# Attention stages with small heads: scores in pairs of different 64-row halves, maxima in pairs behind them

## The chip, the cores and the metric

One Trainium2 chip, one of its cores. The metric is the device time of one execution in microseconds: median of the runs, lower is better. Engines are called TensorE (PE), VectorE (DVE), ScalarE (ACT), GpSimd (POOL) and SyncE (SP).

## The reference

Eight layers on x of 4 x 512 tokens and 256 channels, each adding to x what it makes of the normalised x: a selective scan, a mixture of experts, rotary attention, the same experts, then two attentions of which the kernel makes the stages pattern and latent, other experts, grouped attention with a memory, and the other experts again. What matters here is three attentions whose heads are small:

- rotary and pattern: 16 heads of width 16 each, queries and keys of 512 tokens a batch, four batches. Of each head `softmax(q k^T * scale) v`, where the maximum over the keys is taken off before the exponential.
- grouped: 4 x 8 query heads of width 8 on 8 shared key heads, the same softmax, then a mix with what a memory gives.

## The kernel before, in words

Nine stages run one after the other: mamba, ffn0, rotary, ffn0, pattern, latent, ffn1, grouped, ffn1. Every engine runs its own list of instructions, and semaphores join them. In the three stages named above, the class `Heads` (L931 to L1180) lays out the attention.

**Stacks.** A group is four heads of one batch. There are 16 groups in rotary and in pattern, 32 in grouped. For each, the q of four heads stands in `q_stack` in rows of the 128 partitions: a head takes 64 rows in rotary and pattern (two heads to a tile, two tiles), and 32 in grouped (four heads in one tile). The rows hold high and low parts of q, and a row that carries the negated maximum, so that scores come out with it taken off. Keys stand likewise in `k_stack` in rotary and pattern. In grouped they stand in `k_alone`, one 128-row plane per key head, zero everywhere but in the 32 rows of the head (`k_tiles` set), and a matmul there contracts over all 128 rows.

**Events.** `schedule` (L991) writes one list of events that every engine walks in this order, taking its part of each:

- `ek`, `eq` (L1077, L1078): two matmuls make a stack in PSUM, ScalarE copies it out (L1111, L1115).
- `mx` (L1081): a score matmul with queries on the partitions, 128 x 512; VectorE reduces it to its negated maximum (L1149). Four query tiles of four heads: 16 a group, each of the next group while this one is at its scores.
- `bias` (L1086, L1155): four small matmuls turn the maxima, VectorE adds them into the stack. One a tile.
- `s` (L1090): a score matmul with 128 keys on the partitions; ScalarE takes the exponential into `probs` (L1126).
- `pv` (L1096): the product with v and with a column of ones, four heads side by side in 32 columns each, eight instructions.
- `sums`, `norm`, `o cut`: ScalarE copies the sums out (L1133), VectorE transposes, divides and transposes back (L1160 to L1171), GpSimd cuts it into a high and a low part (L330, L332).

**Units.** A group has four units, one for each tile of 128 keys (kt 0 to 3), so there are 64, 64 and 128 of them. A unit is four `s`, then the `pv` of the unit before. Twelve slots a group, three a unit, hold the other events. Slots 0 and 1 of a unit are shared out behind the four scores: half of slot 0 behind the first, half behind the second, slot 1 behind the third and fourth. Slot 2 comes behind `pv`. The maxima stand ahead in the slots, 1, 3, 3, 2, 2, 2, 3 of them in slots 0, 1, 3, 4, 6, 7, 9, that is 4, 5, 4, 3 by unit. The bias is in slot 10 (with two tiles the first one in slot 5), the norm of the group before in slot 4, the stacks of the group after next in slot 11. Projections of q, k and v, the front of the next batch, output and memory are put into further slots by each stage, mostly into the last slot of a unit.

**Banks.** Scores take PSUM banks 0, 1, 2 in turn: a score waits for the exponential of the third one before it. `pv` sums in bank 6. All else takes 3, 4, 5, 7 in turn: an event waits until the fourth one before it has been read (`free`, L1034). TensorE takes its events strictly in this order, so that a wait holds up all that is behind it.

Of the kernel before, what the change touches and what calls it, by code (L numbers as in the profile page):

```python
# [30 lines left out]
QT = L // P  # L31
# [118 lines left out]
def build(nc, io, out, plan, table):  # L150
    ctx = ExitStack()
    with ctx:
# [774 lines left out]

        AUXB = (3, 4, 5, 7)
        SCORES = (0, 1, 2)

        class Heads:  # L931

# [3 lines left out]
            def __init__(self, alloc, heads, width, rows, khead, scale, q_tile, k_tile, k_tiles, c, C, SEL):  # L936
                self.width, self.rows, self.khead, self.scale = width, rows, khead, scale
                self.q_tile, self.k_tile, self.k_tiles, self.SEL = q_tile, k_tile, k_tiles, SEL
                self.one = c[:, C.whole("one_row")]
                self.per = P // rows  # L940
                self.G4 = heads // 4
                self.NG = NB * self.G4
                self.tiles = 4 // self.per
                self.nkv = len({khead(h) for h in range(heads)})
                self.slots = [[[] for _ in range(12)] for _ in range(self.NG)]
                self.QS = alloc("q_stack", [P, 2, self.tiles, L], F32R)
                self.KS = None if k_tiles else alloc("k_stack", [P, 2, self.tiles, L], F32R)
                self.KZ = alloc("k_alone", [P, 2, self.nkv, L], F32R) if k_tiles else None
                self.MB = alloc("max_cols", [P, 2, QT, P], F32R)
                self.VA = alloc("v_aug", [P, 2, QT, self.nkv, 32])  # L950
                self.PB = alloc("probs", [P, 8, L])
                self.OS = alloc("o_sums", [P, 2, L])
                self.REC = alloc("o_scaled", [P, 2, L])
                self.OH, self.OL = alloc("o_hi", [P, self.G4, L], F32R), alloc("o_lo", [P, self.G4, L], F32R)
# [16 lines left out]
                return evs  # L971

            def maxima(self, g):
                return [("mx", g, t * self.per + i, q) for t in range(self.tiles) for q in range(QT) for i in range(self.per)]

            def k_rows(self, g, h):

                r = slice((h % self.per) * self.rows, (h % self.per + 1) * self.rows)
                if self.k_tiles:
                    return self.KZ[:, (g // self.G4) % 2, self.khead((g % self.G4) * 4 + h), :]  # L980
                return self.KS[r, g % 2, h // self.per, :]

            def q_rows(self, g, h):

                r = slice((h % self.per) * self.rows, (h % self.per + 1) * self.rows)
                return self.QS[:, g % 2, h // self.per, :] if self.k_tiles else self.QS[r, g % 2, h // self.per, :]

            def k_tile_no(self, g, h):
                return self.khead((g % self.G4) * 4 + h) // self.per if self.k_tiles else h // self.per
# [1 line left out]
            def schedule(self, begin, end, reader):  # L991

                for g in range(self.NG):
                    n = g + 1
                    if n < self.NG:
                        mx, had = self.maxima(n), 0
                        for pos, count in ((0, 1), (1, 3), (3, 3), (4, 2), (6, 2), (7, 2), (9, 3)):
                            self.slots[g][pos] = mx[had:had + count] + self.slots[g][pos]
                            had += count
                        if self.tiles > 1:  # L1000
                            self.slots[g][5].insert(0, ("bias", n, 0))
                        self.slots[g][10].append(("bias", n, self.tiles - 1))
                        self.slots[n][4] += [("norm", g), ("o cut", g)]
                    if g + 2 < self.NG:
                        self.slots[g][11] = self.stacks(g + 2) + self.slots[g][11]
                events = begin + self.stacks(0) + self.maxima(0) + [("bias", 0, t) for t in range(self.tiles)] + self.stacks(1)
                units = [(g, kt) for g in range(self.NG) for kt in range(QT)]
                for n in range(len(units) + 1):
                    at = self.slots[units[n][0]][units[n][1] * 3:units[n][1] * 3 + 3] if n < len(units) else [[]] * 3
                    for h in range(4):  # L1010
                        if n < len(units):
                            events.append(("s",) + units[n] + (h,))
                        here = at[h // 2]
                        events += here[len(here) // 2:] if h % 2 else here[:len(here) // 2]
                    if n:
                        events.append(("pv",) + units[n - 1])
                        if units[n - 1][1] == QT - 1:
                            events.append(("sums", units[n - 1][0]))
                    events += at[2]
# [6 lines left out]
                return bank[AUXB[self.aux_no[ev] % len(AUXB)]]  # L1026

            def step_no(self, g, kt, h):
                return (g * QT + kt) * 4 + h

            def scores(self, n):
                return bank[SCORES[n % len(SCORES)]]

# [1690 lines left out]
```

## Time and profile before

| what | value |
|---|---|
| time, median of 3 runs | 4565.31 us (4560.84 to 4579.52) |
| the profiled execution | 4568.12 us |
| its span | 4566.3 us |
| TensorE in use | 3840.6 us (84%) |
| VectorE in use | 2580.8 us (57%) |
| ScalarE in use | 1687.5 us (37%) |
| GpSimd in use | 1353.1 us (30%) |
| granted TensorE clock, mean | 0.912 |

The profile is of one execution. "In use" counts the time in which at least one instruction of the engine is at work. Matmuls are pipelined: the next one starts before the last has ended, so a matmul of 0.39 us can follow another after 0.23 us. What TensorE really takes for one is read from start to start. A row such as `L1096 ... x8` merges instructions of one line that follow without a pause: its time is from the start of the first to the end of the last. The granted clock is the mean over a stretch of the share of full speed that TensorE was given, which at any moment is either 1 or 0.5.

### The profile page before, as it was taken

The page shows a single profiled execution, that of the slowest core. Times are in us where ns is not written, and L with a number is a line of the kernel's source. Part 1 is how long each engine was busy: PE and PEld are TensorE (multiplying, and loading weights), DVE is VectorE, ACT ScalarE, POOL GpSimd, SP SyncE. Part 2 cuts the span into 40 slices and gives each one's busy share as a digit, 9 for nine tenths or more (in the row PEclk, how much of TensorE's full clock was granted, in tenths as well). Part 3 has the DMA queues.
Part 4 walks back from the last instruction along what each step waited for, and adds up shares of the span by engine and source line. Part 5 has one row for each costly group of instructions (what it writes and reads, how often), then busy time and mean ns, then how long its engine had stood idle before and what let it go on. Part 6 is the DMA issues. An engine that isn't in the chain of part 4 may idle for free.

```text
span 4566.3 us, 44420 instructions
## 1 busy us (share of the span) xinstructions
PE 3840.6 (84%) x15840; PEld 2548.4 (56%) x15840; DVE 2580.8 (57%) x4324; ACT 1687.5 (37%) x2807; POOL 1353.1 (30%) x1074
## 2 busy tenths in 40 slices
PE   6869778887978883888889887999878888879999
PEld 4647544435844432555555555788744444457887
DVE  5645366654456652678686765433356766655333
ACT  2433256653235540232323223222245555522222
POOL 3234322214320102333323314444322221143442
PEclk8989889988989976999999998999989999979999
DMA  1010000001000002101000101000000000010000
GB/s 56 1 37 5 29 1 1 1 1 41 1 22 5 5 5 80 28 16 26 18 24 17 26 16 58 18 27 9 16 1 1 1 1 1 1 58 21 25 13 19
DMA packets 32760, 83.27 MB, mean 18 GB/s; under 512 B 6304, under 2 KB 7456, under 8 KB 32288
## 3 DMA queue, kind: packets, MB, share of 16 engines
q1 hardware_dynamic: 32544, 80.44, 5.7%
q8 instruction: 130, 2.13, 0.2%
q14 instruction: 86, 0.70, 0.0%
HBM read 59.44 MB, written 4.19 MB: 14 GB/s over the span
## 4 chain that ended last, share of the span: by engine, by line
PE 54%; DVE 22%; ACT 5%; POOL 3%; issue 2%; DMA 1%; SPq 1%; DVEq 0%; POOLq 0%; ACTq 0%
PE ps L226 11%; PE ps L227 10%; PE ps L228 10%; DVE max_cols L1149 7%; PE ps L1096 5%; PE ps L1935 3%; PE ps L1090 2%; PE ps L296 2%; DVE q_lo L2112 2%; DVE max_cols L2128 2%; PE ps L1081 2%; ACT probs L1126 1%; PE ps L1086 1%; PE ps L800 1%; PE ps L1077 1%
## 5 line engine op out<-in xcount | busy, mean ns | idle before, releaser
L1149 DVE TENSOR_REDUCE max_cols<-ps 128x1 fp32r<-128x512 f32 x1024 | 635.6, 680 | 284.9 <-PE ps L1081 284.1
L1126 ACT ACTIVATE probs<-ps 128x512 f32<-128x512 f32 x1024 | 546.1, 603 | 256.5 <-PE ps L1090 164.6
L754 POOL TENSOR_TENSOR h_lo<-h,h_hi 128x512 fp32r<-128x512 f32 x304 | 392.5, 1291 | 816.6 <-ACT h_hi L834 816.6
L911 DVE TENSOR_TENSOR gated<-silu,ps 128x512 f32<-128x512 f32 x288 | 197.9, 687 | 689.1 <-PE ps L228 665.7
L828 ACT ACTIVATE silu<-ps 128x512 f32<-128x512 f32 x304 | 181.9, 598 | 928.0 <-PE ps L228 927.9
L226 PE MATMUL ps<-xn_hi,w_hi 128*128 128x512 f32 x1216 | 479.5, 394 | 0.0
L227 PE MATMUL ps<-xn_lo,w_hi 128*128 128x512 f32 x1216 | 476.0, 391 | 0.0
L228 PE MATMUL ps<-xn_hi,w_lo 128*128 128x512 f32 x1216 | 475.8, 391 | 0.0
L1096 PE MATMUL ps<-probs,v_aug 128*32 128x512 f32 x2048 | 310.3, 683 | 0.0
L330 POOL CAST o_hi<-o_scaled 128x512 fp32r<-128x512 f32 x64 | 39.1, 612 | 910.1 <-DVE o_scaled L1171 910.1
L1935 PE MATMUL ps<-probs,v_tok 128*128 128x512 f32 x512 | 263.5, 611 | 2.7 <-ACT denominators L1997 2.7
L226 PEld LDWEIGHTS ps<-xn_hi,w_hi 128*128 128x128 f32 x1216 | 231.0, 190 | 49.8 <-issue 1.0
L227 PEld LDWEIGHTS ps<-xn_lo,w_hi 128*128 128x128 f32 x1216 | 230.4, 189 | 49.6 <-issue 1.4
L228 PEld LDWEIGHTS ps<-xn_hi,w_lo 128*128 128x128 f32 x1216 | 230.0, 189 | 48.6
L226 PE MATMUL ps<-h_hi,w_hi 128*128 128x512 f32 x608 | 249.4, 410 | 1.2 <-POOL h_lo L754 1.2
L1090 PE MATMUL ps<-q_stack,k_alone 128*128 128x512 f32 x512 | 213.9, 440 | 31.3 <-ACT probs L1126 29.1
L227 PE MATMUL ps<-h_lo,w_hi 128*128 128x512 f32 x608 | 239.7, 394 | 0.0
L228 PE MATMUL ps<-h_hi,w_lo 128*128 128x512 f32 x608 | 239.6, 394 | 0.0
L1090 PE MATMUL ps<-q_stack,k_stack 64*128 64x512 f32 x512 | 198.8, 485 | 43.3 <-ACT probs L1126 41.2
L1987 ACT ACTIVATE probs<-ps 128x1024 f32<-128x1024 f32 x128 | 131.2, 1025 | 279.1 <-PE ps L1932 278.9
L1081 PE MATMUL ps<-k_alone,q_stack 128*128 128x512 f32 x512 | 201.7, 432 | 37.8 <-ACT q_stack L1115 23.7
L2128 DVE TENSOR_REDUCE max_cols<-ps 128x1 fp32r<-128x512 f32 x256 | 169.2, 682 | 89.6 <-PE ps L1921 89.3
(460 smaller groups left out, 7896.1 us busy)
## 6 DMA issues: line engine op xcount, KB each, us to landing
raw<-in_w_ffn SPq DMA_DIRECT2D x76, 448.0 KB, 3.3
raw<-raw SPq DMA_DIRECT2D x256, 64.0 KB, 2.0
composed_inputs<-in_m_latent SPq DMA_DIRECT2D x1, 5120.0 KB, 15.5
raw<-in_w_mamba SPq DMA_DIRECT2D x8, 448.0 KB, 5.9
raw<-in_w_latent SPq DMA_DIRECT2D x5, 448.0 KB, 16.8
x<-in_x SPq DMA_DIRECT2D x4, 512.0 KB, 6.2
gated_pattern<-gated SPq DMA_DIRECT2D x4, 512.0 KB, 3.1
raw<-gated_pattern SPq DMA_DIRECT2D x4, 512.0 KB, 4.3
```

Of the source, the lines that this page charges most:

```text
L226: nc.tensor.matmul(psum, wh, xh, start=start, stop=False)
L227: nc.tensor.matmul(psum, wh, xl, start=False, stop=False)
L228: return nc.tensor.matmul(psum, wl, xh, start=False, stop=stop)
L754: nc.gpsimd.tensor_tensor(HL[:, b % 3, :], hb[:, b % 2, :], HH[:, b % 3, :].bitcast(F32), ALU.subtract).then_inc(G.sem, G.step((s, ev)))
L911: nc.vector.tensor_tensor(ga if routed(i) else hb[:, i % 2, :], sg[:, i % 2, :], bank[2 + i % 2], ALU.mult).then_inc(V.sem, V.step((s, "ga ...
L1081: last = nc.tensor.matmul(self.psum(ev), self.q_rows(g, h)[:, q * P:(q + 1) * P], self.k_rows(g, h), start=True, stop=True)
L1090: last = nc.tensor.matmul(self.scores(self.step_no(g, kt, h)), self.k_rows(g, h)[:, kt * P:(kt + 1) * P], self.q_rows(g, h), start=True, s ...
L1096: last = nc.tensor.matmul(bank[6][32 * h:32 * h + 32, :], self.VA[:, (g // self.G4) % 2, kt, self.khead((g % self.G4) * 4 + h), :], self.P ...
L1126: nc.scalar.activation(self.PB[:, n % 8, :], self.scores(n), ACT.Exp, scale=self.scale).then_inc(A.sem, A.step((s, ("exp", n))))
L1149: nc.vector.tensor_reduce(self.MB[:, self.tile_of(g, h) % 2, q, col:col + 1], self.psum(ev), op=ALU.max, axis=AX.X, negate=True).then_inc( ...
L1935: last = nc.tensor.matmul(bank[6 + i], VT[:, (g // HP) % 2, kt, 64 - 64 * i:192 - 64 * i], PB[:, (g * QT + kt) % 2, i, :], start=kt == 0, ...
L2128: nc.vector.tensor_reduce(MB[:, q, 32 * i:32 * i + 1], bank[slot(ev)], op=ALU.max, axis=AX.X, negate=True).then_inc(V.sem, V.step((s, ev)))
```

## The change

Four edits in `Heads`.

1. **Order of heads** (`turn`). A unit's scores come in two pairs, each of one head in rows 0 to 63 and one in rows 64 to 127: heads 0, 1 and 2, 3 in rotary and pattern, 0, 2 and 1, 3 in grouped. The maxima go through the heads in the same order, and score banks and probabilities are numbered by it (`step_no`).
2. **Rows** (`half`). In grouped a score or maximum matmul now reads the 64 rows that hold its head (and another one's, zero in `k_alone`), not all 128. In rotary and pattern the rows stay as they were.
3. **Places of the maxima** (`FIRST_MX`). They are out of the slots. Behind the first pair of scores of a unit stand 2, 4, 2, 2 of them (kt 0 to 3), behind the second pair 2, 2, 2, 0: 4, 6, 4, 2 by unit.
4. **Slots.** Slot 0 of a unit comes whole behind the first pair of scores and its maxima, slot 1 behind the second. Slot 2 stays behind `pv`.

```diff
         AUXB = (3, 4, 5, 7)
         SCORES = (0, 1, 2)
+        FIRST_MX = (0, 2, 4, 8, 10, 12, 14, 16, 16)
...
+                self.turn = (0, 2, 1, 3) if k_tiles else (0, 1, 2, 3)
...
             def maxima(self, g):
-                return [("mx", g, t * self.per + i, q) for t in range(self.tiles) for q in range(QT) for i in range(self.per)]
+                turn = self.turn[:self.per]
+                return [("mx", g, t * self.per + i, q) for t in range(self.tiles) for q in range(QT) for i in turn]
+
+            def half(self, h):
+
+                n = (h // 2 if self.k_tiles else h) % 2
+                return slice(n * 64, n * 64 + 64)
 
             def k_rows(self, g, h):
 
-                r = slice((h % self.per) * self.rows, (h % self.per + 1) * self.rows)
+                r = self.half(h)
                 if self.k_tiles:
-                    return self.KZ[:, (g // self.G4) % 2, self.khead((g % self.G4) * 4 + h), :]
+                    return self.KZ[r, (g // self.G4) % 2, self.khead((g % self.G4) * 4 + h), :]
                 return self.KS[r, g % 2, h // self.per, :]
 
             def q_rows(self, g, h):
 
-                r = slice((h % self.per) * self.rows, (h % self.per + 1) * self.rows)
-                return self.QS[:, g % 2, h // self.per, :] if self.k_tiles else self.QS[r, g % 2, h // self.per, :]
+                return self.QS[self.half(h), g % 2, h // self.per, :]
...
                     if n < self.NG:
-                        mx, had = self.maxima(n), 0
-                        for pos, count in ((0, 1), (1, 3), (3, 3), (4, 2), (6, 2), (7, 2), (9, 3)):
-                            self.slots[g][pos] = mx[had:had + count] + self.slots[g][pos]
-                            had += count
...
-                    for h in range(4):
-                        if n < len(units):
-                            events.append(("s",) + units[n] + (h,))
-                        here = at[h // 2]
-                        events += here[len(here) // 2:] if h % 2 else here[:len(here) // 2]
+                    for k in range(2) if n < len(units) else ():
+                        g, kt = units[n]
+                        one, two = (("s", g, kt, h) for h in self.turn[2 * k:2 * k + 2])
+                        mx = self.maxima(g + 1)[FIRST_MX[2 * kt + k]:FIRST_MX[2 * kt + k + 1]] if g + 1 < self.NG else []
+                        events += [one, two] + mx + at[k]
...
             def step_no(self, g, kt, h):
-                return (g * QT + kt) * 4 + h
+                return (g * QT + kt) * 4 + self.turn.index(h)
```

## Rows read from the trace of the kernel before

**Rows 1.** The page: busy time by engine; the chain that ended last, by line.

```profile
PE 3840.6 (84%) x15840; PEld 2548.4 (56%) x15840; DVE 2580.8 (57%) x4324; ACT 1687.5 (37%) x2807; POOL 1353.1 (30%) x1074
...
PE ps L226 11%; PE ps L227 10%; PE ps L228 10%; DVE max_cols L1149 7%; PE ps L1096 5%; PE ps L1935 3%; PE ps L1090 2%; PE ps L296 2%; DVE q_lo L2112 2%; DVE max_cols L2128 2%; PE ps L1081 2%; ACT probs L1126 1%; PE ps L1086 1%; PE ps L800 1%; PE ps L1077 1%
```

**Rows 2.** Windows of the rotary, pattern and grouped stage: start:end, length, busy (instructions), clock.

```profile
616.00:1018.00 402.00, 344.82 (x1545) 165.35 (x1544) 262.49 (x438) 245.99 (x434) 86.12 (x78) 0.91 0.00 1
1331.00:1702.00 371.00, 316.78 (x1498) 154.23 (x1497) 227.45 (x381) 197.40 (x369) 38.62 (x36) 0.89 0.01 5
3354.00:3990.00 636.00, 536.79 (x2474) 275.11 (x2472) 428.80 (x722) 356.79 (x654) 126.75 (x111) 0.94 0.00 1
```

**Rows 3.** The chain of waits inside the grouped stage (3354 to 3990), by line.

```profile
by line: DVE max_cols L1149 25.1%; PE ps L1096 14.7%; PE ps L1081 9.3%; PE ps L1090 8.9%; PE ps L1086 2.8%; ACT k_alone L1111 2.6%; DVE o_turned L1160 2.5%; DVE o_scaled L1171 2.5%; ACT q_stack L1115 2.1%; PE ps L1077 2.0%; issue 1.9%; PE p
```

**Rows 4.** TensorE's waits there: who <- for whom: us in total, times, longest.

```profile
PE ps L1086 <- DVE max_cols L1149: 30.9, 28, 1.4
PE ps L1090 <- ACT probs L1126: 29.1, 11, 4.0
PE ps L1081 <- ACT q_stack L1115: 19.1, 22, 4.9
```

**Rows 5.** Waits of all engines there, the row of VectorE's maxima.

```profile
DVE max_cols L1149 <- PE ps L1081: 129.3, 77, 8.1
```

**Rows 6.** Timeline of TensorE, grouped stage: start, us, engine line op out<-in, [idle <-releaser].

```profile
3625.28 0.39 PE L1078 MATMUL ps<-heads_lo,h_grouped_hi 128*128 128x512 f32 x1
3625.51 0.62 PE L1090 MATMUL ps<-q_stack,k_alone 128*128 128x512 f32 x2
3626.36 0.50 PE L1081 MATMUL ps<-k_alone,q_stack 128*128 128x512 f32 x1 [0.23 <-ACT q_stack L1115]
...
3627.94 1.06 PE L1096 MATMUL ps<-probs,v_aug 128*32 128x512 f32 x8
...
3633.58 0.48 PE L1090 MATMUL ps<-q_stack,k_alone 128*128 128x512 f32 x1
...
3635.04 0.39 PE L1090 MATMUL ps<-q_stack,k_alone 128*128 128x512 f32 x1
...
3635.59 1.06 PE L1096 MATMUL ps<-probs,v_aug 128*32 128x512 f32 x8
3636.59 0.50 PE L1090 MATMUL ps<-q_stack,k_alone 128*128 128x512 f32 x1
```

**Rows 7.** The same for a unit of the rotary stage.

```profile
808.00 0.39 PE L1078 MATMUL ps<-heads_lo,h_rotary_hi 128*128 128x512 f32 x1
808.32 0.50 PE L1090 MATMUL ps<-q_stack,k_stack 64*128 64x512 f32 x2
808.66 0.40 PE L1081 MATMUL ps<-k_stack,q_stack 64*128 64x512 f32 x2
...
809.82 0.49 PE L1090 MATMUL ps<-q_stack,k_stack 64*128 64x512 f32 x1 [0.54 <-ACT probs L1126]
809.82 0.72 PE L1081 MATMUL ps<-k_stack,q_stack 64*128 64x512 f32 x2
810.48 1.06 PE L1096 MATMUL ps<-probs,v_aug 128*32 128x512 f32 x8
```

**Rows 8.** Timeline of VectorE beside rows 6.

```profile
3624.05 0.69 DVE L1155 TENSOR_TENSOR q_stack<-q_stack,ps 128x512 fp32r<-128x512 f32 x1 [0.75 <-PE ps L1086]
3626.89 2.48 DVE L1149 TENSOR_REDUCE max_cols<-ps 128x1 fp32r<-128x512 f32 x4 [2.15 <-PE ps L1081]
3630.37 3.08 DVE L1149 TENSOR_REDUCE max_cols<-ps 128x1 fp32r<-128x512 f32 x5 [0.99 <-PE ps L1081]
...
3635.55 4.24 DVE L1149 TENSOR_REDUCE max_cols<-ps 128x1 fp32r<-128x512 f32 x7
```

**Rows 9.** A 20 us window in the grouped stage, columns as in rows 2.

```profile
3480.00:3500.00 20.00, 14.95 (x68) 7.41 (x66) 12.39 (x21) 9.94 (x19) 8.68 (x7) 0.83 0.01 2
```

**Rows 10.** Timeline of TensorE, grouped stage: the eight matmuls of L1096 at half clock.

```profile
3510.01 1.65 PE L1096 MATMUL ps<-probs,v_aug 128*32 128x512 f32 x8
```

## The prediction

> **What bounds the kernel now.** I read the page first: TensorE is busy 84% of the span and its matmuls fill most of the chain that ended last, but the lines of the change (scores L1090, maxima L1081, their VectorE reduction L1149, L1096 behind them) come to 16% of it [rows 1]. Then the three stages with small heads by window: 402, 371 and 636 us, 1409 us in all [rows 2]. In each of them TensorE is in use 84 to 86%, VectorE 61 to 67%, ScalarE 53 to 61%: nothing is full, so order and latency decide. The chain inside the grouped stage has the VectorE maxima as its largest item, 25.1%, then L1096 with 14.7%, and the two kinds of matmul that are to be paired with 9.3% and 8.9% [rows 3]. TensorE's own waits there are 30.9 us for VectorE's last maximum before a bias, 29.1 us for an exponential before a score, 19.1 us for the copied q stack before a maximum [rows 4]. VectorE in turn waited 129.3 us, 77 times, for a matmul of a maximum [rows 5]: the two hand the work to and fro.
>
> **What a pair is worth by itself.** In the grouped stage eight matmuls of a unit start 0.23 us apart whatever they are (3625.28 to 3625.51; six steps from 3633.58 to 3635.04 make 1.46) [rows 6]. In the rotary stage, where 64-row halves exist already, two scores start together at 808.32 and two maxima together at 808.66 [rows 7]. So a pair costs one slot, and in the grouped stage 1024 matmuls would need 512 slots: 512 x 0.23 = 118 us less of matmul issue. In rotary and pattern half of that has been had: scores and maxima alternate in halves there too, and only those that fall on the same half are apart.
>
> **What stays of it.** A unit is four scores, its maxima, then four products with v (L1096). There are three score banks, so the fourth score waits for the exponential of the first. In the rotary unit of the rows, where everything is side by side, the fourth score starts 1.50 us after the first (it waited 0.54 us for ScalarE), then comes 0.33 for the last maximum and 0.33 to L1096: 2.16 us from first score to L1096 [rows 7]. The grouped unit at 3633.58 has no pair at all and takes 3635.59 - 3633.58 = 2.01 us, with its fourth score at 1.46 [rows 6]. The unpaired maxima cost it nothing, because they filled the time in which the fourth score could not have started anyway. For such a unit the change saves nothing, and could cost 0.15 us. Only the first unit of each group is longer now: 3627.94 - 3625.51 = 2.43 us, because its first maximum waits until 0.85 us for the q stack and the rest runs in single file behind it [rows 6]. Side by side it comes to about 2.16, a gain of 0.27 x 32 groups = 9 us (none, if VectorE is late anyway; 0.43 x 32 = 14 if the 1.50 of the rotary row, in which ScalarE was late, shrinks by 0.16).
>
> **VectorE's side.** Reductions run back to back at 4.24 / 7 = 0.606 us [rows 8]; sixteen a group are 9.7 us, and neither their number nor their time changes. In the group of the rows VectorE works without a pause from 3630.37 to 3639.8, through the five maxima of the second unit, the norm (3633.56 to 3635.55) and the seven of the last two units. The bias that follows must wait for it. The change shares the maxima 4, 6, 4, 2 over the four units instead of 4, 5, 4, 3: the same twelve stand between the start of the second unit and the bias, so where VectorE is continuous the group ends no sooner. Where it had run dry before the last unit, one maximum fewer is left to do: 0.6 us less. Of the 77 waits, 32 are the first of a group, 2.15 us each as after the row at 3624.05 (69 us), which pairing doesn't touch, since they end with the ScalarE copy; 60 us in 45 waits are left, of which I put half the groups at the full 0.6 us: 16 x 0.6 = 10 us in the grouped stage. Rotary and pattern have 32 groups together: the same half, 10 us. Ends: none and 38 us.
>
> **Costs of the order.** Four banks serve maxima and everything else but scores and L1096. The sixth maximum of the second unit needs VectorE to have read the second one: 0.33 + 0.5 until the first is there, 2 x 0.6 for two reductions, so about 2.03 us after the first score, where the last maximum of the rotary row starts at 1.50 + 0.33 = 1.83: the unit becomes 0.2 us longer. It counts where TensorE is late, say in half of 64 groups: 32 x 0.2 = 6 us (0 to 13). A switch between full-height and 64-row matmuls is seen too: from the last full one to the first score it is 0.32 us in rotary (808.00 to 808.32) against 0.23 in the grouped stage (3625.28 to 3625.51) [rows 6, 7]. In the grouped stage about 60 of 128 units have a full matmul right ahead of the first score (q stack 32, v 16, memory, output): 60 x 0.09 = 5 us. Behind L1096, with its 32 columns, a switch is paid today as well, so it adds nothing. The Trainium skill, TensorEngine Tiling (Array Packing), Key Properties, says that a change of tiling mode, not just of tile, drains the engine; by that rule the switches cost on every crossing, and the trace's 0.09 us is what such a crossing shows.
>
> ScalarE, GpSimd and DMA get the same instructions. That q and k of a grouped head are now read from 64 rows, not 128, leaves out rows in which k_alone is zero. The other events of a unit stand up to two matmuls earlier or later than before; bias and norm keep their slots.
>
> Order alone: -9 - 10 + 3 + 5 = -11 us grouped, -10 + 3 = -7 us in the other two: -18 us.
>
> **The clock.** The granted clock is 0.94 in the grouped stage, 0.91 in rotary and 0.89 in pattern, where pairs are already common [rows 2]; within the grouped stage, a stretch in which TensorE was in use only 14.95 of 20 us had 0.83 [rows 9]. These are means over the two levels, 2.4 and 1.2 GHz. The change takes up to 118 us of matmul issue out of the grouped stage and leaves waits in its place, so I expect it to come down to the other two, 0.90: 2 x 0.04 x 636 = 51 us more at 1.2 GHz. At that level L1096's eight took 1.65 us against 1.06 [rows 6, 10]. What it costs lies between 0 (VectorE holds the pace) and half of that time (TensorE does); TensorE's lines add up to 38% of the chain [rows 3], which would give 0.2, and a late TensorE makes the others late too, so 0.3: +15 us, and 0.01 in the other stages (2 x 0.01 x 773 x 0.3 = 5): +20 us. Ends: 0, and 2 x 0.11 x 636 x 0.5 = 70 us if the whole grouped stage goes to 0.83. The Trainium skill, TensorE: Matmul & The Clock Gate, Part 1, says that the throttled state is the default and activity releases it. The stretches agree in sign, and the rule speaks against a change whose point is to keep the array less long in use.
>
> **Sum.** The profiled execution took 4568.12 us (span 4566.3), 2.8 us above the median of the three, 4565.31. 4568.1 - 18 + 20 = 4570, on the median's footing 4568: no change that can be told (0.5%, 23 us, is about what a measurement of this kernel can tell).
>
> **The rivals.**
> *TensorE sets the pace after all.* The chain puts 9.3 + 8.9% of 636 us = 116 us on the paired matmuls of the grouped stage, and halving them gives 58 us, plus some 10 in the other stages, with the clock's 20 against it: 4565 - 48 = 4517; with less gain 4535. For it: the chain's shares, and that TensorE's three largest waits are only 79 of 636 us [rows 4]. Against it: the unit of 2.01 us without a pair.
> *The clock falls far: slower.* With waits where maxima stood, a slow stretch doesn't refill the array enough to be released, and slow stretches follow each other. At 0.83 in the grouped stage the price is 42 (at 0.3) to 70 us, less 18 for the order: 4589 to 4617. It decides from about 0.86 down: 2 x 0.08 x 636 x 0.4 = 41 us is the order's 18 and the 23 of the bound. For it: rows 9. Against it: at 1.2 GHz the same work fills twice the time, which brings the use back.
> *The pairs don't pair.* The fourth score of a unit starts 0.8 us behind the third in the rotary row, held by the exponential; if the third always runs alone, and the grouped stage's starts stay 0.23 apart because both read the same k bank, only the costs remain, 3 + 3 + 5 = 11 us, and no clock loss: 4576.
>
> **How the numbers follow.** Forecast (order small, clock eats it) 0.44, its own range 4545 to 4588; TensorE sets the pace 0.25; the clock falls far 0.22; no pairs 0.09. Range 4520 to 4612: most of the faster rival and the slower one up to the lesser clock. Faster by over 0.5%: 0.22 + 0.05 of the forecast's edge = 0.27. Slower: 0.20 + 0.06 of forecast and no pairs = 0.26. Within: 0.47.
>
> **What would show it.** Right: in the grouped stage starts of two scores within 0.01 us; L1096 still 2.0 to 2.2 us after the first score in plain units; the wait of L1090 for probs grown from 29 us by some 40; VectorE busy as before; clock near 0.90. Wrong: the grouped stage under 600 us with VectorE over 72% in use (first rival), or its clock under 0.86 and the stage over 655 us (second), or score starts 0.23 apart (third).

## The result and the profile after

The changed kernel takes 4602.24 us in the median of six runs (4597.01 to 4618.7), the kernel before 4568.98 (4560.84 to 4579.52) beside it. The medians are 33 us apart, the ratio is 1.0081 (1.0061 to 1.0102): slower, clear of noise. That lies inside the range, but 34 us over the forecast of 4568, which was for no change that can be told. The range holds it because it took in part of the rival "the clock falls far", priced at 4589 to 4617, and the time is that rival's.

The page of the profiled execution (span 4597.0 us): busy time by engine, the chain by line, the group of the maxima. Lines behind L1020 have moved by three: maxima are L1084 and L1152, scores L1093, exponentials L1129, products with v L1099, the bias L1089.

```profile
PE 3862.4 (84%) x15840; PEld 2506.5 (55%) x15840; DVE 2582.7 (56%) x4324; ACT 1679.3 (37%) x2807; POOL 1352.1 (29%) x1074
...
PE ps L226 10%; PE ps L227 10%; PE ps L228 10%; DVE max_cols L1152 6%; PE ps L1099 5%; PE ps L1938 3%; PE ps L1093 3%; PE ps L296 2%; DVE q_lo L2115 2%; DVE max_cols L2131 2%; PE ps L1084 2%; ACT probs L1129 2%; PE ps L1089 1%; PE ps L800 1%; PE ps L1080 1%
...
L1152 DVE TENSOR_REDUCE max_cols<-ps 128x1 fp32r<-128x512 f32 x1024 | 634.8, 681 | 311.5 <-PE ps L1084 311.0
```

TensorE is in use 84% as before and VectorE has the same 2582 us. What has moved is in the stages. Here are windows of the three attentions, from the first maximum to the last L1099 (start:end, length, busy of PE, PEld, DVE, ACT, POOL with instructions, clock, DMA share, GB/s), first in the kernel before, these windows being a little wider than those of [rows 2]:

```profile
601.00:1023.00 422.00, 363.87 (x1593) 175.15 (x1596) 273.43 (x456) 250.54 (x441) 86.12 (x78) 0.89 0.00 1
1316.00:1701.00 385.00, 329.59 (x1531) 162.03 (x1530) 238.99 (x400) 200.65 (x373) 38.62 (x36) 0.88 0.01 5
3342.00:3989.00 647.00, 546.58 (x2490) 281.07 (x2494) 438.76 (x738) 356.52 (x653) 126.75 (x111) 0.94 0.00 1
```

and the same of the kernel after:

```profile
605.00:1027.00 422.00, 368.21 (x1593) 178.95 (x1596) 273.51 (x456) 250.38 (x442) 86.16 (x79) 0.88 0.00 1
1323.00:1693.00 370.00, 322.08 (x1530) 159.55 (x1530) 239.14 (x400) 198.17 (x372) 38.59 (x36) 0.92 0.01 5
3330.00:4019.00 689.00, 572.43 (x2494) 238.58 (x2494) 437.58 (x738) 350.77 (x654) 126.38 (x111) 0.81 0.00 1
```

Rotary takes 422 us in both, pattern 370 for 385, grouped 689 for 647. The grouped stage loses 42 us, its clock falls from 0.94 to 0.81, and VectorE and ScalarE do the same work. Pattern's 15 us are no gain of the change, as the experiments show. (From the clock's own transitions in these windows, in us at the lower level: before 94, 94 and 84; after 101, 58 and 259.) The chain inside the grouped stage, to be read against [rows 3]:

```profile
by line: DVE max_cols L1152 22.5%; PE ps L1099 18.2%; PE ps L1093 10.1%; PE ps L1084 7.7%; PE ps L1089 3.4%; PE ps L1080 2.5%; ACT k_alone L1114 2.4%; DVE o_turned L1163 2.2%; DVE o_scaled L1174 2.2%; ACT probs L1129 2.1%; PE ps L296 1.9%; 
```

VectorE's maxima have gone from 25.1 to 22.5%, L1099, which the change doesn't touch, from 14.7 to 18.2%: of a window of 677 us that is 123 us, where it was 93 of 636. The same eight matmuls take 1.93 us at the lower clock and 1.06 at the higher, as rows further down show. The waits of TensorE in this window, against [rows 4], and VectorE's for the maxima, against [rows 5] (us in total, times, longest):

```profile
PE ps L1093 <- ACT probs L1129: 39.0, 43, 4.5
PE ps L1089 <- DVE max_cols L1152: 25.5, 29, 1.6
PE ps L1084 <- ACT q_stack L1118: 16.7, 14, 5.0
```

```profile
DVE max_cols L1152 <- PE ps L1084: 160.5, 62, 9.4
```

The wait for an exponential has grown by 10 us, the one for the last maximum has shrunk by 5, and VectorE waits 31 us longer for its maxima. The timeline of TensorE in the grouped stage shows why neither is the main thing (start, length, line, form):

```profile
3600.34 1.93 PE L1099 MATMUL ps<-probs,v_aug 128*32 128x512 f32 x8
3602.20 0.79 PE L1093 MATMUL ps<-q_stack,k_alone 64*128 64x512 f32 x2
3602.79 0.63 PE L1084 MATMUL ps<-k_alone,q_stack 64*128 64x512 f32 x2
3603.22 1.06 PE L1093 MATMUL ps<-q_stack,k_alone 64*128 64x512 f32 x2
3604.80 0.66 PE L1089 MATMUL ps<-h_grouped_hi,max_cols 128*128 128x128 f32 x4 [0.52 <-DVE max_cols L1152]
...
3607.05 0.49 PE L1093 MATMUL ps<-q_stack,k_alone 64*128 64x512 f32 x2
3607.80 0.57 PE L1084 MATMUL ps<-k_alone,q_stack 64*128 64x512 f32 x2 [0.26 <-ACT q_stack L1118]
3608.14 0.65 PE L1093 MATMUL ps<-q_stack,k_alone 64*128 64x512 f32 x2
3608.39 0.63 PE L1084 MATMUL ps<-k_alone,q_stack 64*128 64x512 f32 x2
3608.95 1.07 PE L1099 MATMUL ps<-probs,v_aug 128*32 128x512 f32 x8
...
3610.74 0.50 PE L1093 MATMUL ps<-q_stack,k_alone 64*128 64x512 f32 x2
3611.07 0.63 PE L1084 MATMUL ps<-k_alone,q_stack 64*128 64x512 f32 x4
3611.53 0.88 PE L1093 MATMUL ps<-q_stack,k_alone 64*128 64x512 f32 x2
3612.33 1.07 PE L1084 MATMUL ps<-k_alone,q_stack 64*128 64x512 f32 x2
3613.33 0.64 PE L1099 MATMUL ps<-probs,v_aug 128*32 128x512 f32 x4
```

The unit at 3607.05 is the one that [rows 6] has at 3625.51. Its first two scores start together, its first two maxima start 0.10 us apart, 0.75 after the first score, when the q stack has been copied, and L1099 comes after 1.90 us, where it came after 2.43. The unit at 3610.74 has six maxima, and L1099 comes after 2.59 us. Its last maximum waits for VectorE's reading: L1084 at 3612.33 is two matmuls with 0.60 us between their starts. Up to 3603.9 the clock is at its lower level. There the two pairs at 3602.20 and 3602.79 are 0.59 apart, the next 0.43, and the eight of L1099 at 3600.34 take 1.93 us. Of some 32 units of each kind (first to fourth of a group), those wholly at full clock take 3.80, 4.95, 3.80 and 4.84 us in the mean from first score to first score (13, 15, 21 and 10 units), a group of 17.4; in the kernel before 4.25, 4.24, 4.28 and 5.51 (23, 26, 26 and 26 units), 18.3. In the units at full clock the change gains. It is at full clock less often. (These are not the same units in both kernels, so the 0.9 us a group is a hint, not a measurement.)

Fewer matmuls ran side by side than the prediction counted on. Of the 1024 scores and maxima of the grouped stage, 257 start within 0.02 us of the one ahead, where 512 had been reckoned, and 116 more within 0.2 us; by slots of 0.23 us that saves TensorE 71 us of issue, not 118. The first two scores of a unit start together in 124 of 128 units, the third and fourth in 4: the fourth waits for the exponential of the first, and comes 0.39 us behind the third in the median.

One stretch shows that the use share doesn't tell the clock. The window from 3460 to 3480, before:

```profile
3460.00:3480.00 20.00, 18.22 (x99) 10.13 (x94) 13.74 (x24) 12.02 (x24) 1.89 (x2) 1.00 0.01 1
```

and after:

```profile
3460.00:3480.00 20.00, 18.17 (x85) 7.56 (x81) 12.73 (x22) 10.25 (x20) 1.89 (x2) 0.83 0.00 1
```

TensorE counts as in use for 18.2 us in both, with 99 matmuls started in one and 85 in the other, and the clock is 1.00 and 0.83. Two matmuls that overlap count once, and a matmul at the lower clock lasts longer (L1093 0.79 us, not 0.49, in the rows above), so that fewer of them fill the same time.

### The profile page after: what moved, and what is told of

Read it like the earlier page. It is cut to its first block, busy times and chain, and to the rows that moved or that the text cites. A ratio compares the mean times of both kernels' runs of the same rounds, so it can differ in the third digit from the quotient of the medians.

```text
span 4597.0 us, 44420 instructions
## 1 busy us (share of the span) xinstructions
PE 3862.4 (84%) x15840; PEld 2506.5 (55%) x15840; DVE 2582.7 (56%) x4324; ACT 1679.3 (37%) x2807; POOL 1352.1 (29%) x1074
## 4 chain that ended last, share of the span: by engine, by line
PE 54%; DVE 21%; ACT 6%; POOL 3%; issue 2%; DMA 1%; SPq 1%; DVEq 0%; POOLq 0%; ACTq 0%
PE ps L226 10%; PE ps L227 10%; PE ps L228 10%; DVE max_cols L1152 6%; PE ps L1099 5%; PE ps L1938 3%; PE ps L1093 3%; PE ps L296 2%; DVE q_lo L2115 2%; DVE max_cols L2131 2%; PE ps L1084 2%; ACT probs L1129 2%; PE ps L1089 1%; PE ps L800 1%; PE ps L1080 1%
## 5 line engine op out<-in xcount | busy, mean ns | idle before, releaser
L1152 DVE TENSOR_REDUCE max_cols<-ps 128x1 fp32r<-128x512 f32 x1024 | 634.8, 681 | 311.5 <-PE ps L1084 311.0
L1129 ACT ACTIVATE probs<-ps 128x512 f32<-128x512 f32 x1024 | 536.7, 603 | 272.8 <-PE ps L1093 268.6
L1099 PE MATMUL ps<-probs,v_aug 128*32 128x512 f32 x2048 | 331.5, 725 | 0.0
L1093 PE MATMUL ps<-q_stack,k_stack 64*128 64x512 f32 x512 | 183.9, 488 | 54.4 <-ACT probs L1129 54.0
L1093 PE MATMUL ps<-q_stack,k_alone 64*128 64x512 f32 x512 | 190.7, 557 | 41.1 <-ACT probs L1129 39.0
L1084 PE MATMUL ps<-k_alone,q_stack 64*128 64x512 f32 x512 | 172.1, 500 | 48.0 <-ACT q_stack L1118 21.3
```

The source lines that it names most:

```text
L1084: last = nc.tensor.matmul(self.psum(ev), self.q_rows(g, h)[:, q * P:(q + 1) * P], self.k_rows(g, h), start=True, stop=True)
L1093: last = nc.tensor.matmul(self.scores(self.step_no(g, kt, h)), self.k_rows(g, h)[:, kt * P:(kt + 1) * P], self.q_rows(g, h), start=True, s ...
L1099: last = nc.tensor.matmul(bank[6][32 * h:32 * h + 32, :], self.VA[:, (g // self.G4) % 2, kt, self.khead((g % self.G4) * 4 + h), :], self.P ...
L1129: nc.scalar.activation(self.PB[:, n % 8, :], self.scores(n), ACT.Exp, scale=self.scale).then_inc(A.sem, A.step((s, ("exp", n))))
L1152: nc.vector.tensor_reduce(self.MB[:, self.tile_of(g, h) % 2, q, col:col + 1], self.psum(ev), op=ALU.max, axis=AX.X, negate=True).then_inc( ...
```

## The experiments

Each was timed in five rounds beside the kernel before, whose medians there were 4562 to 4567 us. Ratios are to that kernel, with their 95% intervals; "stage" is the length of the grouped attention in the profiled execution, "low" its time at the lower clock. The profiled execution is one of the runs and can lie off the median: 13 us above it in e_fill2, 8 in e_fill_more, 8 below it in e_even.

| kernel | median us | ratio | stage us | clock | low us |
|---|---|---|---|---|---|
| before | 4565 | 1 | 647 | 0.94 | 84 |
| after | 4602 | 1.0081 (1.0061, 1.0102) | 689 | 0.81 | 259 |
| e_grouped_old | 4565 | 0.9995 (0.9984, 1.0007) | 653 | 0.92 | 98 |
| e_order | 4570 | 1.0012 (1.0000, 1.0023) | 659 | 0.93 | 89 |
| e_rows | 4626 | 1.0128 (1.0109, 1.0147) | 713 | 0.79 | 293 |
| e_fill2 | 4581 | 1.0028 (1.0017, 1.0038) | 671 | 0.86 | 183 |
| e_fill_more | 4594 | 1.0053 (1.0032, 1.0073) | 671 | 0.89 | 145 |
| e_fill2_full | 4605 | 1.0085 (1.0063, 1.0107) | 693 | 0.88 | 173 |
| e_even | 4681 | 1.0254 (1.0230, 1.0279) | 729 | 0.77 | 333 |
| e_early | 4578 | 1.0034 (1.0018, 1.0050) | 671 | 0.84 | 220 |
| e_old_fill | 4549 | 0.9960 (0.9945, 0.9975) | 647 | 0.95 | 68 |
| e_best | 4578 | 1.0033 (1.0018, 1.0048) | 666 | 0.92 | 101 |
| e_before_fill | 4541 | 0.9946 (0.9929, 0.9963) | 645 | 0.95 | 66 |
| e_pair_fill | 4566 | 0.9999 (0.9983, 1.0014) | 666 | 0.87 | 170 |

**Which part, which stage.** Four kernels with rotary and pattern as after make a square of the grouped stage: contracts over 128 or 64 rows, old or new order. `e_grouped_old` has neither part there.

```diff
-                self.turn = (0, 2, 1, 3) if k_tiles else (0, 1, 2, 3)
+                self.turn = (0, 1, 2, 3)
...
+                        for pos, count in ((0, 1), (1, 3), (3, 3), (4, 2), (6, 2), (7, 2), (9, 3)) if self.k_tiles else ():
...
+                if self.k_tiles:
+                    return slice(0, P)
```

> The grouped stage keeps the order and the 128-row contracts of before; rotary and pattern are as after. If all the loss sits in the grouped stage (my reading of the two traces: attention of rotary 422 to 422 us, pattern 384 to 370, grouped 647 to 688), this kernel takes 4545 to 4560, faster than before, with the grouped attention at 647 us and clock 0.93 there. The rival, that pattern's 14 us are chance of the clock's phase, gives 4565 to 4575.

It took 4565.0, ratio 0.9995. The loss is all in the grouped stage. That pattern gains 14 us is only in part so: its windows

```profile
605.00:1027.00 422.00, 367.20 (x1592) 178.19 (x1596) 273.31 (x456) 250.22 (x441) 86.15 (x78) 0.88 0.00 1
1320.00:1696.00 376.00, 327.21 (x1527) 162.99 (x1530) 239.31 (x400) 199.36 (x373) 38.57 (x36) 0.90 0.01 5
3342.00:3995.00 653.00, 552.00 (x2494) 283.53 (x2494) 439.15 (x738) 357.25 (x654) 126.80 (x111) 0.92 0.00 1
```

have pattern at 376 with clock 0.90, and the median shows nothing gained. The rival of the clock's phase was right, and the traces together show what the phase is worth. In after, e_grouped_old, e_order, e_rows, e_fill2, e_fill_more and e_fill2_full, pattern has the same list of matmuls. It takes 371 us with 58 us at the lower clock in two of them, then 376 (71 and 72 low), 379 (75), 382 (88) and 385 (88). Its longest is

```profile
1323.00:1708.00 385.00, 335.96 (x1530) 164.00 (x1530) 238.72 (x400) 198.76 (x373) 38.52 (x36) 0.89 0.01 5
```

A line through the seven has 0.43 us of stage for each us at the lower clock, with the matmuls the same. So pattern's 385 us before and 370 after lie at the two ends of what one list of matmuls gives.

`e_order` is the new order with 128 rows.

```diff
             def half(self, h):
+                if self.k_tiles:
+                    return slice(0, P)
```

> As after, but in the grouped stage scores and maxima contract over all 128 rows: the new order and the new places of the maxima without anything side by side. Clock theory (the loss comes from TensorE being so little in use that the clock falls): clock in the grouped attention back to 0.92 or more, from 0.81, and the stage 630 to 660 us, so 4550 to 4580 in all, faster than after although 512 slots of 0.23 us are added. Rival (the order costs: the sixth maximum, scores ahead of maxima): the stage stays at 680 us or more and the whole at 4600 or more.

It took 4570.0, 32 us less than after, although no two of its 1024 scores and maxima start together, which is 71 us more of matmul issue by the count above:

```profile
3340.00:3999.00 659.00, 555.10 (x2494) 281.57 (x2493) 438.69 (x738) 351.85 (x653) 126.61 (x111) 0.93 0.00 1
```

The clock is back at 0.93. The order by itself costs little (5 us over e_grouped_old, at the edge of the noise). The rival, that the order is what costs, falls. After and e_order differ in the rows that a matmul reads and, by that, in what runs side by side; no kernel has 64 rows with nothing side by side, so the two are not told apart here.

`e_rows` is the old order with 64 rows.

```diff
+                        for pos, count in ((0, 1), (1, 3), (3, 3), (4, 2), (6, 2), (7, 2), (9, 3)) if self.k_tiles else ():
...
                 n = (h // 2 if self.k_tiles else h) % 2
                 return slice(n * 64, n * 64 + 64)
```

> The order of before in the grouped stage, with contracts over 64 rows; pairs come about only by chance of the halves. Rotary and pattern are as after. Clock theory: between the two, clock 0.85 to 0.90 in the grouped attention, the stage at 650 to 680 us. Rival (the order costs): the stage at 620 to 645 us, since pairs save TensorE time and the old order is kept.

```profile
3334.00:4047.00 713.00, 589.79 (x2490) 254.32 (x2492) 437.90 (x738) 354.36 (x653) 126.33 (x111) 0.79 0.00 1
```

It took 4625.8, 61 us more than e_grouped_old, at a clock of 0.79: more than either theory allowed. The expectation took it that few pairs would come about by chance, but 227 of the 1024 scores and maxima start with the one ahead, nearly the 257 of after, and the clock falls as far. So the 64 rows are the whole loss, and the new order takes back 24 us of the 61. The units that are wholly at full clock again make a shorter group than before (17.7 us, from 10, 21, 20 and only 4 units), which points at the level of the clock for the rest.

**Put the work back where it costs nothing.** `e_fill2` is after with matmuls of zeros, added onto the open sums of bank 6, while TensorE waits for the exponential.

```diff
+                    if self.k_tiles and h == 3 and kt in (0, 2, 3) and g + kt:
+                        for _ in range(2):
+                            nc.tensor.matmul(bank[6], self.NIL[0:64, :], self.QS[0:64, g % 2, 0, :], start=False, stop=False)
```

> As after, with two more matmuls (64 rows of zeros by 512 columns, added onto the sums of bank 6, which they leave as they are) ahead of the fourth score of a unit of the grouped stage, in three units of four: 190 x 0.23 = 44 us more TensorE work, put where TensorE waits for the exponential. Clock theory: clock in the grouped attention rises from 0.81 to 0.88 or more and the kernel gets faster by 15 to 40 us in spite of the work, 4560 to 4590. Rival (clock is a symptom, TensorE waits for VectorE and ScalarE as it must): the same 4602 or up to 20 us slower.

```profile
3344.00:4015.00 671.00, 563.12 (x2680) 260.79 (x2684) 438.78 (x738) 350.24 (x654) 126.38 (x111) 0.86 0.00 1
```

4580.9 us: 21 less than after, for 190 matmuls more. Time at the lower clock went from 259 to 183 us. Nothing else in the kernel was made shorter, so this is the sharpest evidence for the clock as cause. One microsecond less at the lower level was worth 18 / 76 = 0.24 us of the stage, the added work included.

`e_fill_more` has three ahead of the fourth score, three ahead of each bias and two ahead of a group's first maximum.

> As the kernel with two zero matmuls ahead of the fourth score (4581 us), but more of them in the grouped stage: three ahead of the fourth score in three units of four, three ahead of each bias (TensorE waits there for VectorE's last maximum) and two ahead of the first maximum of a group (it waits for the q stack). Some 420 in place of 190. Clock theory: clock in the grouped attention from 0.864 to 0.90 or more, the time down again, 4550 to 4575. Rival (two were enough, the rest is work on the path): 4580 to 4600.

```profile
3352.00:4023.00 671.00, 586.77 (x2932) 296.45 (x2932) 438.64 (x738) 353.16 (x654) 126.59 (x111) 0.89 0.00 1
```

A miss: the clock did rise, to 0.89, but the stage stayed at 671, and the median is 4593.7, as the rival had it. What the clock gave back (38 us less at the lower level, some 10 us by the price of e_fill2) the added zeros probably took on TensorE's path; which of the three places costs it was not tried. Where the 13 us between the medians of e_fill_more and e_fill2 arise isn't shown either: the profiled executions have the stage equally long.

`e_fill2_full` is e_fill2 with zeros over 128 rows.

> As the kernel with two zero matmuls ahead of the fourth score, but these over 128 rows, not 64. If what holds the clock up is the time in which the array streams, it does the same as 64 rows: 4581 and 0.86, with up to 10 us for the switches of tile height. If the number of rows in use counts, the clock rises above 0.88 and the time falls below 4575.

```profile
3335.00:4028.00 693.00, 602.59 (x2681) 254.49 (x2684) 440.91 (x738) 357.30 (x654) 126.34 (x111) 0.88 0.00 1
```

4605.0 us. The clock is that of e_fill2 within 0.02 (173 and 183 us low), the stage 22 us longer. The timelines tell where: a 64-row score, two zeros, then the fourth score, with 128 rows

```profile
3647.46 0.39 PE L1104 MATMUL ps<-q_stack,k_alone 64*128 64x512 f32 x1
3647.79 0.73 PE L1046 MATMUL ps<-q_stack,nil 128*128 128x512 f32 x2
3648.45 0.50 PE L1104 MATMUL ps<-q_stack,k_alone 64*128 64x512 f32 x1
3648.45 0.73 PE L1095 MATMUL ps<-k_alone,q_stack 64*128 64x512 f32 x2
```

and with 64, where the zeros follow the third score after 0.23, not 0.33, and the fourth score no longer shows as a row of its own:

```profile
3643.72 0.65 PE L1097 MATMUL ps<-q_stack,k_alone 64*128 64x512 f32 x2
3643.95 0.62 PE L1063 MATMUL ps<-q_stack,nil 64*128 64x512 f32 x2
3644.21 0.60 PE L1088 MATMUL ps<-k_alone,q_stack 64*128 64x512 f32 x2
```

The first 128-row zero starts 0.33 behind the score, the second 0.33 behind the first (though they have the same height), the next score 0.33 behind that, and of the two maxima there the second again 0.33 behind the first. (Two matmuls in a row of 0.73 us are 0.33 apart, two in a row of 0.62 are 0.23 apart.) At one height each step is 0.23. So a switch of height costs 0.1 us ahead of the first matmul of the new height and 0.1 behind it, 0.2 in all. In the rows of after above it is the same: 3610.74 to 3611.07 is 0.33, and the two pairs of maxima from there to 3611.53 take 0.23 each. 95 units with two switches make 38 us of issue, of which the stage is 22 us longer; the rest fell, it seems, into TensorE's waits. The prediction had 0.09 a switch, the part ahead alone.

**Where the maxima stand.** `e_even` and `e_early` are after with other shares by unit, 4, 4, 4, 4 (the first added line) and 6, 6, 4, 0 (the second).

```diff
-        FIRST_MX = (0, 2, 4, 8, 10, 12, 14, 16, 16)
+        FIRST_MX = (0, 2, 4, 6, 8, 10, 12, 14, 16)
+        FIRST_MX = (0, 4, 6, 10, 12, 14, 16, 16, 16)
```

> As after, but the maxima are spread 4, 4, 4, 4 over the four units, not 4, 6, 4, 2. By my term for the sixth maximum and that for one maximum less in the last unit, the two about cancel (-6 and +5 us in the grouped stage): within 8 us of after, 4594 to 4610. Rival (pairs want VectorE's queue filled early): 4612 or more.

```profile
600.00:1047.00 447.00, 369.22 (x1598) 179.13 (x1596) 274.52 (x456) 251.62 (x442) 86.32 (x79) 0.86 0.00 1
1340.00:1728.00 388.00, 324.30 (x1526) 162.23 (x1528) 238.44 (x399) 198.91 (x372) 38.59 (x36) 0.89 0.01 5
3365.00:4094.00 729.00, 588.88 (x2494) 244.25 (x2494) 438.08 (x738) 349.94 (x654) 126.26 (x111) 0.77 0.00 1
```

The largest miss of all: 4680.6, 78 us over after, in every stage (447, 388 and 729 us for 422, 370 and 689). TensorE's wait for the last maximum before a bias is

```profile
PE ps L1089 <- DVE max_cols L1152: 56.2, 32, 3.7
```

twice the 25.5 us of after. 64 groups x 2 maxima x 0.61 us are 78 us, as if the two maxima that moved into the last unit each prolonged every group by their whole length. That is not shown: the whole execution also has 123 us more at the lower clock than after's (1075 for 952 us), 74 of them in the grouped stage, and the wait above is 31 us longer in a grouped stage that is 40 us longer. The two causes were not parted, and that the numbers meet may be chance. The prediction's term for a maximum taken out of the last unit had 0.6 us in half the groups only.

> As after, with the maxima of a group spread 6, 6, 4, 0 over its units, in all three stages. Moving two of them from the second unit into the last cost 78 us (64 groups x 2 x 0.61). If the maxima that are late in a group set its end, taking the last two out of the fourth unit gives something back: at most 78 us, 20 to 50 if VectorE is then continuous in part of the groups, 4550 to 4582. Rival (with two in the last unit VectorE had no slack to use): 4590 to 4610.

```profile
3331.00:4002.00 671.00, 560.18 (x2494) 237.25 (x2492) 436.65 (x738) 350.53 (x653) 126.35 (x111) 0.84 0.00 1
```

4577.8 us, 24 less than after. So after's 4, 6, 4, 2 is not the best with pairs. Here too the time at the lower clock moves with it, 220 us for 259. It is no general rule: in `e_best` below earlier maxima cost 29 us.

**A version that beats both.** `e_old_fill` is e_grouped_old with zeros in the waits of all three stages. The expectation names two ahead of a group's first maximum as well; the kernel that ran did not have them.

```diff
+                if kind == "s" and ev[3] == 3 and ev[2] in (0, 2, 3) and ev[1] + ev[2] and not self.k_tiles:
+                    self.fill(ev[1], 2)
+                elif kind == "bias" and ev[1]:
+                    self.fill(ev[1] - 1, 3)
```

> The kernel whose grouped stage is as before while rotary and pattern are paired (4565 us), with zero matmuls in all three stages: three ahead of each bias, two ahead of the first maximum of a group, and in rotary and pattern two ahead of the fourth score. If the clock of 0.88 to 0.91 in rotary and pattern costs as much per microsecond as that in the grouped stage, 170 us at half clock fall to under 90 and the kernel takes 4535 to 4555, faster than both. Rival (what is filled there lies on TensorE's path, since these stages have more projection work between the waits): 4565 to 4580.

4549.1 us, 0.9960: faster than before, and 16 us less than e_grouped_old. Rotary and pattern:

```profile
605.00:1031.00 426.00, 396.06 (x1778) 206.38 (x1777) 273.23 (x456) 251.80 (x442) 86.43 (x79) 0.90 0.00 1
1324.00:1685.00 361.00, 342.23 (x1710) 182.82 (x1714) 239.47 (x400) 198.13 (x373) 38.63 (x36) 0.96 0.01 5
```

Against e_grouped_old pattern gains 15 us and rotary loses 4. The grouped stage, with zeros ahead of each bias alone, goes from 653 to 647 us (68 us low for 98).

`e_best` is e_old_fill with maxima 6, 6, 4, 0 in rotary and pattern, 5, 6, 4, 1 in grouped.

```diff
-        FIRST_MX = (0, 2, 4, 8, 10, 12, 14, 16, 16)
+        FIRST_MX = (0, 4, 6, 10, 12, 14, 16, 16, 16)
...
-((0, 1), (1, 3), (3, 3), (4, 2), (6, 2), (7, 2), (9, 3))
+((0, 2), (1, 3), (3, 3), (4, 3), (6, 2), (7, 2), (9, 1))
```

> The fastest so far (grouped in the old order with 128 rows, pairs in rotary and pattern, zero matmuls in the waits: 4549 us) with earlier maxima: 6, 6, 4, 0 in rotary and pattern, 5, 6, 4, 1 in grouped. If late maxima set the end of a group there as well: 4505 to 4535. Rival: 4545 to 4555.

It took 4578.1. Rotary went from 426 to 438 us, its clock hardly changed (0.91), and grouped from 647 to 666, with the clock at 0.92 for 0.95 (101 us low for 68). The first unit of a group, with six maxima in place of four, needs 2.60 us from the first score to the product with v, against 1.91 (medians of 15 units each in rotary, clock full). The expectation took e_even's slope to run on; it doesn't.

`e_before_fill` is the same zeros in the kernel before, none of the change in it.

> The kernel before, in all three stages, with the zero matmuls of the fastest version (three ahead of each bias, and in rotary and pattern two ahead of the fourth score of three units in four). If the pairs of rotary and pattern are worth nothing and the 16 us came from the clock alone: 4545 to 4555, as with pairs. Rival (pairs leave room in which the zeros cost nothing, here they stand on TensorE's path): 4558 to 4570.

```profile
602.00:1024.00 422.00, 386.45 (x1778) 201.55 (x1780) 273.61 (x456) 251.87 (x442) 86.23 (x79) 0.92 0.00 1
1318.00:1676.00 358.00, 330.00 (x1714) 176.47 (x1712) 239.00 (x399) 198.16 (x372) 38.60 (x36) 0.98 0.01 5
3316.00:3961.00 645.00, 567.36 (x2587) 293.44 (x2587) 439.14 (x738) 356.55 (x653) 126.62 (x111) 0.95 0.00 1
```

4540.6 us, 0.9946 (0.9929 to 0.9963): the fastest of all, 25 us less than before. Pattern has 358 us for 385, with a clock of 0.98 for 0.88. The first expectation comes out, on its good side. Beside the 0.9960 of e_old_fill (the intervals overlap) pairs in rotary and pattern add nothing.

`e_pair_fill` pairs all three stages, has maxima 6, 6, 4, 0 in grouped, and zeros: two ahead of the fourth score everywhere, three ahead of a bias in rotary and pattern.

```diff
+                        first_mx = (0, 4, 6, 10, 12, 14, 16, 16, 16) if self.k_tiles else FIRST_MX
...
+                for _ in range(count if (kind_ == "s" or not self.k_tiles) else 0):
```

> Everything paired as after, the maxima of the grouped stage 6, 6, 4, 0, two zero matmuls ahead of the fourth score in all three stages and three ahead of each bias in rotary and pattern. If the gains of the single steps add up (4602, less 24 for early maxima of which two thirds are the grouped stage's, less 21 for the zeros there, less 16 for those in rotary and pattern): 4545 to 4560, level with the kernel before or a little better. Rival (early maxima already fill the wait that the zeros fill): 4565 to 4585.

```profile
3318.00:3984.00 666.00, 573.36 (x2680) 264.93 (x2682) 436.67 (x738) 350.04 (x653) 126.36 (x111) 0.87 0.00 1
```

4565.6, level with before and 6 us outside the better expectation, at the edge of the rival's. The steps do not add up: the grouped stage keeps 170 us at the lower clock, and is 21 us longer than in e_before_fill.

## Why the prediction came out as it did

- **What a pair is worth.** Right for a pair: starts 0.003 us apart in the grouped stage, no slot for the second. Wrong in the count: 257 starts saved, not 512, and 71 us of issue, not 118, mainly because the fourth score still waits for the exponential.
- **What stays of it.** Mis-sized, too low. From the first score to L1099 the first unit of a group gained 0.53 us, not 0.27 (medians of units at full clock, 2.43 to 1.90), and a plain one, the third of a group, 0.22 (2.06 to 1.84), where the prediction had nothing.
- **Places of the maxima.** The term was a gain of 20 us (32 x 0.6, over all three stages) against a cost of 6 (32 x 0.2). In the grouped stage's second unit, with its sixth maximum, L1099 comes 0.34 us later at full clock (2.28 to 2.62), not 0.2. e_even's 78 us are 0.6 in all 64 groups for each maximum that goes into the last unit, the clock's part included. But the step back from 4, 5, 4, 3 to 4, 6, 4, 2 gave nothing in e_order. What makes the one dear and the other free is left open.
- **Switches.** Half of it: 0.09 was predicted and 0.1 found ahead of a switch, but another 0.1 follows behind it, so that the 60 switches cost up to 12 us, not 5.
- **Order alone, -18 us.** Rotary and pattern: -2 predicted with the clock's part, 0.9995 (0.9984 to 1.0007) measured, -2 us by the medians of 4565 and 4567. Grouped: -11. The measured 42 us hold 175 us more at the lower clock. At 0.24 to 0.43 each (e_fill2; pattern over seven kernels) that is 42 to 75 us, so order and pairs have given something between nothing and 33 us. The units at full clock point at the upper end, 0.9 x 32 = 29 us. The -11 lies between; the runs do not fix it closer.
- **The clock: the step that failed.** It was put at 0.90 for the grouped stage, from rotary and pattern, 51 us more at the lower level; it came to 0.81, 175 us. The price per microsecond, 0.3, lies within what was found (0.24 to 0.43), so it is the fall of the clock that the sum had at under a third. By the prediction's own signs (clock under 0.86 and the stage over 655 us) the second rival came out, not the forecast. Rotary and pattern were the wrong neighbours to take: their units are longer (402 and 371 us for 64, against 636 for 128) and hold more matmuls (some 24 a unit, against 19). That this is what keeps their clock up was not tried; that putting matmuls back between the pairs of the grouped stage raises it was (e_fill2). The stretch at 0.83 [rows 9] was the better guide, and it stood there as the rival's.
- **The rivals.** TensorE as the pace-setter fell: e_order has 71 us more of matmul issue than after and is faster. That pairs don't pair fell for the first two scores of a unit, but held for the third and fourth, as that rival had it.
- **The sum and the readings.** 4570 less 2.8 is 4567, not 4568, and in the rotary unit of [rows 7] the fourth score starts 0.92 us behind the third, not 0.8; neither changes the forecast. That the time lies in the range is owed to the rival's share in it; the forecast itself was for no change, and the kernel became slower beyond the noise.

What the Trainium skill says on this, TensorE: Matmul & The Clock Gate, Part 1 (throttled by default, released by activity), agrees with these runs: the clock is 0.93 in e_order, where every score and maximum has a slot to itself, and 0.81 in after. It was weighed in the right direction and at under a third of its size.

## What to carry to other kernels

Where no engine is full, taking matmul work away on TensorE can cost more through the granted clock than it saves, so look at the clock by stage before the use share, and price the time at the lower level from rows. A matmul of zeros in a wait, a few tenths of a microsecond each, is a cheap test of whether the clock is what costs, and may be kept as a gain: 25 us here. One execution can mislead about a stage: the same matmuls of pattern took 371 to 385 us, by the time that they had at the lower clock. Where VectorE's work stood in a group moved the time by 24 us down to 78 up, and no place was best in all kernels, so it has to be tried.

## What had not been expected of the hardware

Letting 257 of 1024 matmuls start with the one ahead, some 71 us less of issue in 647 us, brought the granted clock from 0.94 to 0.81 and made the stage longer by 42 us. Matmuls whose weights are all zero count for the clock: 0.88 to 0.98 in pattern with e_before_fill. Zeros over 128 rows raised it hardly more than zeros over 64 (173 and 183 us at the lower level, from 259). And a switch between 64 and 128 rows costs 0.1 us ahead of the first matmul of the new height and another 0.1 behind it, whichever height comes first.
